# Dilated-convolution attention and a selective scan on one core: projection weights loaded a batch ahead into a second place, last-stage loads cut into 16 rows and one row, image margins cleared only

## The reference

```
# layer 0: four convolutions (1x1, and 3x3 with dilations 6, 12, 18), 32 channels each
branches = [relu(bn(conv(x, w, pad=p, dilation=d))) for w, p, d in ((w1,0,1),(w2,6,6),(w3,12,12),(w4,18,18))]
Q = wq . concat(branches) + bq      # 16 channels
K = wk . x + bk                     # 16 channels
V = wv . x + bv                     # 128 channels
Qn, Kn = Q/|Q|, K/|K|               # over channels
tailor = 1 / (N + Qn . (sum(Kn) + eps))
out = gamma * (sum(V) + Qn . (Kn V^T)) * tailor
# layer 1: on tokens x = out, D_MODEL 128, D_INNER 256, D_STATE 16
xh, z = split(x @ W_in);  xh = silu(causal_conv2(xh))
dt, Bm, Cm = softplus((xh W_x)[:8] W_dt + b_dt), (xh W_x)[8:24], (xh W_x)[24:40]
h = exp(dt*A) * h + dt*Bm*xh        # for each token, 256 x 16 states
y = (sum over states of h*Cm + xh*D) * silu(z)
y = silu(group_norm(y @ W_out, 4 groups)) + x
```

## Time and profile before

| | |
|---|---|
| median of 3 runs | 16281.83 us (16277.56 to 16301.75) |
| the profiled execution's own time | 16276.23 us |
| its span | 16274.4 us |
| busy: PE, DVE, POOL, ACT | 87%, 86%, 80%, 62% of the span |
| stage A, stages F and start of B, B, C | about 0 to 2440, to 2490, to 16157, to 16274 us |

### The profile page before, as it was taken

How to read it: one execution, slowest core, us unless ns; L and a number is a source line. 1 busy time by engine, 2 the same in 40 slices (tenths; PEclk the granted TensorE clock), 3 DMA queues, 4 the chain that set the end, 5 groups by cost and what they waited for, 6 DMA issues and landing times. The chain is left out here.

```text
span 16274.4 us, 144588 instructions
## 1 busy us (share of the span) xinstructions
PE 14161.2 (87%) x40704; PEld 5407.5 (33%) x40704; DVE 13974.3 (86%) x13537; ACT 10107.5 (62%) x14054; POOL 13069.0 (80%) x5647
## 2 busy tenths in 40 slices
PE   8999997888888888888888888888888888888886
PEld 3333332333333333333333333333333333333332
DVE  1222228999999999999999999999999999999997
ACT  2222225666666666666666666666666676666675
POOL 0000007999999999999999999999999999999996
PEclk9999998999999999999999999999999999999997
DMA  1111104444445545444455454454544444545544
GB/s 50 42 39 44 39 26 151 171 161 169 170 172 180 180 168 180 173 178 171 175 182 181 168 180 173 176 182 164 182 178 172 177 176 175 182 167 181 180 173 172
DMA packets 560359, 2505.37 MB, mean 154 GB/s; under 512 B 58695, under 2 KB 171063, under 8 KB 293448
## 3 DMA queue, kind: packets, MB, share of 16 engines
q1 hardware_dynamic: 549272, 2477.68, 42.9%
q10 hardware_dynamic: 10288, 18.44, 0.4%
HBM read 2325.32 MB, written 170.57 MB: 153 GB/s over the span
## 5 line engine op out<-in xcount | busy, mean ns | idle before, releaser
L794 POOL TENSOR_TENSOR hc<-h,c_all 128x1024 f32<-128x1024 f32 x4096 | 9531.7, 2359 | 574.0 <-DVE h L1161 496.1
L1031 PE MATMUL y_ps<-hc,ident 128*128 128x512 f32 x16392 | 8392.7, 664 | 1127.8 <-POOL hc L794 1127.6
L892 ACT ACTIVATE d_a<-dt,a_neg 128x512 f32<-128x512 f32 x8194 | 5596.1, 689 | 4081.4 <-DVE h L1161 4055.4
L1161 DVE TENSOR_TENSOR_SCAN h<-d_a,h,dbx_v 128x512 f32<-128x512 f32 x5456 | 6622.0, 1262 | 10.4 <-DVE dbx_v L1148 1.1
L1031 PEld LDWEIGHTS y_ps<-hc,ident 128*128 128x128 f32 x16392 | 3362.3, 211 | 6055.1 <-issue 4172.5
L1148 DVE TENSOR_TENSOR dbx_v<-dtx_ps,b_all 128x1024 f32<-128x1024 f32 x2816 | 3313.7, 1206 | 61.0 <-issue 26.2
L1161 DVE TENSOR_TENSOR_SCAN h<-d_a,h,dbx_p 128x512 f32<-128x512 f32 x2480 | 3027.7, 1262 | 10.8 <-issue 0.4
L783 POOL TENSOR_TENSOR dbx_p<-dtx,b_all 128x1024 f32<-128x1024 f32 x1280 | 3002.3, 2355 | 23.8 <-DVE h L1161 0.8
L480 POOL MEMSET ident_f<- 128x128 f32 x1 | 0.2, 205 | 2417.5 <-POOLq L45 2417.5
L273 PE MATMUL conv_ps<-image,w_taps 128*32 128x512 f32 x11520 | 1777.7, 594 | 0.0
L363 DVE RECIPROCAL k_inv<-k_nrm 128x4 f32<-128x4 f32 x256 | 45.5, 178 | 1774.2 <-ACT k_nrm L215 1774.2
(11 more groups left out here) (143 smaller groups left out, 9228.5 us busy)
## 6 DMA issues: line engine op xcount, KB each, us to landing
b_all<-bc_dram SPq DMA_DIRECT2D x1028, 1024.0 KB, 6.3
c_all<-bc_dram SPq DMA_DIRECT2D x1025, 1024.0 KB, 5.0
o_dram<-o_sb SPq DMA_DIRECT2D x257, 256.0 KB, 6.2
o_c<-o_dram SPq DMA_DIRECT2D x220, 256.0 KB
out<-r_c SPq DMA_DIRECT2D x220, 256.0 KB, 7.9
image<-in_x SPq DMA_DIRECT2D x91, 512.0 KB, 4.1
un<-un_dram SPq DMA_DIRECT2D x736, 34.0 KB
bc_dram<-low_bc SPq DMA_DIRECT2D x257, 64.0 KB, 4.6
```

Of the source, the lines that this page charges most:

```text
L794: nc.gpsimd.tensor_tensor(hc[:, n % HC], h[:, n], c_all[:, n // CG % 2, n % CG].unsqueeze(1).broadcast_to([128, 2, CH]), ALU.mult).then_in ...
L892: nc.scalar.activation(d_a[:, half], dt[:, p, half], ACT.Exp, scale=a_neg[:, half, n:n + 1]).then_inc(a_done, 1)
L1031: last = nc.tensor.matmul(y_ps[:, half], ident[:], hc[:, n % HC, half], start=False, stop=(n == S - 1))
L1161: nc.vector.tensor_tensor_scan(h[:, n, half], d_a[:, half], dbx, zero_col[:] if first else h[:, n, half, CH - 1:CH], ALU.mult, ALU.add).th ...
```

## The change

1. **Stage A, margins.** The clearing of the whole `image` becomes four clears: 18 rows above, 18 columns left, 18 columns right, 18 rows below. The four loads of the first image no longer wait for the clears.
2. **Stage A, waits.** PE's one wait per batch becomes several. In the first batch it waits for each of the four loads on a semaphore of its own, before chunks 0, 2, 10 and 18. In later batches it waits for the 13 pieces before chunk 0 and for the last 24 rows before chunk 20.
3. **Stage B, weights.** `w_xz` gets a second place, and the batches take turns. The second batch's weights are loaded in the first body. In the last body of batch b the weights of batch b+2 are loaded, into the place that batch b used. PE waits on one of two semaphores.
4. **Stage C, loads.** Each 17-row load becomes one of 16 rows and one of one row. Only the two batches' matrices are loaded instead of eight. The matrices and the first part of `u_t` are issued by ACT, ahead of its square root. SP issues two loads of `o_t` first, then the second part of `u_t`. The group norm's parameters get a semaphore of their own, so DVE no longer waits for the matrices.

```diff
-            sp.wait_ge(cleared, 6)
             for i in range(4):
                 rows = slice(i * 32, i * 32 + 32)
                 sp.dma_start(image[:, PAD + 32 * i:PAD + 32 * i + 32, PAD:PAD + W],
-                             t["x"][0, :, rows, :]).then_inc(x_loaded, 16)
-
+                             t["x"][0, :, rows, :]).then_inc(x_first[i], 16)
+
+            sp.wait_ge(cleared, CLEARED)
...
-                                 t["x"][b + 1, :, rest:H, :]).then_inc(x_loaded, 16)
+                                 t["x"][b + 1, :, rest:H, :]).then_inc(x_rest, 16)
...
-        def loaded(eng, b):
-
-            eng.wait_ge(x_loaded, 16 * 4 + b * (16 * (PIECES - 2)))
+        def loaded(eng, b, r):
+
+            if b == 0:
+                for i in range(4):
+                    if r == max(0, (32 * i - max(DIL) - ROWS) // ROWS):
+                        eng.wait_ge(x_first[i], 16)
+            elif r == 0:
+                eng.wait_ge(x_loaded, 16 * b * (PIECES - 3))
+            elif r == ((PIECES - 3) * PIECE - max(DIL) - ROWS) // ROWS:
+                eng.wait_ge(x_rest, 16 * b)
...
-            pool.memset(image[:], 0.0).then_inc(cleared, 1)
+            pool.memset(image[:, 0:PAD], 0.0).then_inc(cleared, 1)
+            pool.memset(image[:, PAD:PAD + H, 0:PAD], 0.0).then_inc(cleared, 1)
+            pool.memset(image[:, PAD:PAD + H, PAD + W:WP], 0.0).then_inc(cleared, 1)
+            pool.memset(image[:, PAD + H:WP], 0.0).then_inc(cleared, 1)
...
-        w_xz = sb("w_xz", [64 + KU, 2 * DI])
+        w_xz = sb("w_xz", [64 + KU, 2, 2 * DI])
...
-                if last:
-                    sp.dma_start(w_xz[0:K2], w_dram[bass.ds(b + 1, 1)].rearrange("o k c -> (o k) c")
-                                 ).then_inc(w_loaded, 16)
+                if km == 0:
+                    sp.dma_start(w_xz[0:K2, 1], w_dram[1]).then_inc(w_loaded[1], 16)
+                elif last and b + 2 <= B:
+                    sp.dma_start(w_xz[0:K2, b % 2], w_dram[b + 2]).then_inc(w_loaded[b % 2], 16)
...
-                after(pe, "w_loaded", 16 * batch + 16)
+                after(pe, f"w_loaded{batch % 2}", 16 * (batch // 2) + 16)
...
-        gm = sb("gm_c", [128, B, C])
+        gm = sb("gm_c", [128, 2, C])
...
+        def load_u(eng, i):
+
+            b, j0 = parts[i]
+            c0 = (b * SLOTS + 1) * CH
+            for g in range(groups):
+                for rows in (slice(0, M), slice(M, KU)):
+                    eng.dma_start(u_t[32 * g + rows.start:32 * g + rows.stop, i, j0:],
+                                  un_dram[rows, c0:c0 + N].rearrange("k (j g n) -> k j g n", g=groups, n=CH)[:, j0:, g]
+                                  ).then_inc(u_in[i], 16)
...
+            load_o(0)
+            load_o(1)
+            load_u(sp, 1)
+            for k in range(2, len(blocks)):
+                load_o(k)
...
+            for g in range(groups):
+                for rows in (slice(0, M), slice(M, KU)):
+                    act.dma_start(gm[32 * g + rows.start:32 * g + rows.stop],
+                                  gmat_dram[B - 2:B, rows].rearrange("b k c -> k b c")).then_inc(gm_in, 16)
+            load_u(act, 0)
             act.wait_ge(step, STEPS_BEFORE_ROOT)
```

More of the change, by code:

```diff
@@ L35 @@
 PIECES = H // PIECE
+CLEARED = 9
 HC = 4
@@ L98, in phase_a @@
         pads_stored = sem("pads_stored")
+        x_first = [sem(f"x_first{i}") for i in range(4)]
         x_loaded = sem("x_loaded")
+        x_rest = sem("x_rest")
         conv_done = sem("conv_done")
@@ L202, in _ @@
             act.wait_ge(set_up, 5)
-            act.wait_ge(cleared, 6)
+            act.wait_ge(cleared, CLEARED)
             def relu(b, r, p):
@@ L251, in _ @@
             pe.wait_ge(weights, 16 * 7)
-            pe.wait_ge(cleared, 6)
+            pe.wait_ge(cleared, CLEARED)
             pe.sem_inc(q_mm, 1)
@@ L299, in _ @@
             for b in range(0, B):
-                loaded(pe, b)
                 for r in range(NCH + 1):
@@ L305, in _ @@
                     if r < NCH:
+                        loaded(pe, b, r)
                         kv(b, r, p)
@@ L339, in _ @@
             nc.vector.tensor_tensor(bn_shift[:], bn[:, 1:2], bn_mi[:], ALU.subtract).then_inc(set_up, 1)
-            dve.wait_ge(cleared, 6)
+            dve.wait_ge(cleared, CLEARED)
             dve.sem_inc(v_done, 2)
@@ L599, in phase_b @@
         u_c = un[64:64 + KU]
-        gm_c = w_xz[64:64 + KU].rearrange("k (s c) -> k s c", c=C)
+        gm_c = w_xz[64:64 + KU, 0].rearrange("k (s c) -> k s c", c=C)
         d_a = ps("d_a", [128, 2, CH])
@@ L616, in phase_b @@
         weights, consts, ready, built = stage("weights"), stage("consts"), stage("ready"), stage("built")
-        w_loaded = stage("w_loaded")
+        w_loaded = [stage("w_loaded0"), stage("w_loaded1")]
         un_in = [stage("un_in0"), stage("un_in1")]
@@ L683, in _ @@
             load_un(2 * CH, 1)
-            sp.dma_start(w_xz[0:K2], w_dram[0]).then_inc(w_loaded, 16)
+            sp.dma_start(w_xz[0:K2, 0], w_dram[0]).then_inc(w_loaded[0], 16)
             after(sp, "rows_done", 1)
@@ L755, in _ @@
             after(sp, "bc_stored", 16 * (B * NCH + 1))
-            after(sp, "w_loaded", 16 * (B + 1))
+            after(sp, "w_loaded0", 16 * (B // 2 + 1))
+            after(sp, "w_loaded1", 16 * (B // 2))
             for p in range(2):
@@ L992, in inner, with gated @@
                 after(pe, "dt_done", km + 1)
-                nc.tensor.matmul(p_ps[:, 1 - half], w_xz[0:K2, 128 * half:128 * half + 128], un[0:K2, p],
+                nc.tensor.matmul(p_ps[:, 1 - half], w_xz[0:K2, batch % 2, 128 * half:128 * half + 128], un[0:K2, p],
                                  start=True, stop=True).then_inc(xh_mm[half], 1)
-            def gated(km, p, half):
+            def gated(km, batch, p, half):
                 after(pe, f"xh_silu{half}", km + 2)
-                nc.tensor.matmul(p_ps[:, 1 - half], w_xz[0:K2, DI + 128 * half:DI + 128 * half + 128], un[0:K2, p],
+                nc.tensor.matmul(p_ps[:, 1 - half], w_xz[0:K2, batch % 2, DI + 128 * half:DI + 128 * half + 128], un[0:K2, p],
                                  start=True, stop=True).then_inc(z_mm[half], 1)
@@ L1062, in _ @@
             inner(-1, 1, 0, 0, 1)
[L1063 to L1064 removed]
+            gated(-1, 0, 0, 0)
+            gated(-1, 0, 0, 1)
             project_x(-1, 0)
@@ L1078, in body @@
                 add_state(km - 1, 15)
-                gated(km, q, 0)
-                gated(km, q, 1)
+                gated(km, batch, q, 0)
+                gated(km, batch, q, 1)
                 add_skip(km, p)
@@ L1312, in phase_c, with load_o @@
         blocks = [(b, j, k) for k, (b, j) in enumerate(blocks)]
-        first_of = [sum(NCB - j0 for _, j0 in parts[:i]) for i in range(len(parts) + 1)]
         part_of = [i for i, (_, j0) in enumerate(parts) for _ in range(j0, NCB)]
         groups = CB // CH
+        def load_u(eng, i):
[6 more added lines that the diff above has]
+                                  ).then_inc(u_in[i], 16)
         @block.sync
         def _(sp):
-            sp.dma_start(gn[:], t["gn"]).then_inc(small_in, 16)
-            for g in range(groups):
-                sp.dma_start(gm[32 * g:32 * g + KU], gmat_dram.rearrange("b k c -> k b c")).then_inc(small_in, 16)
-            def load_u(i):
-                b, j0 = parts[i]
-                if i >= 2:
-                    sp.wait_ge(res_mm, first_of[i - 1])
-                c0 = (b * SLOTS + 1) * CH
-                for g in range(groups):
-                    sp.dma_start(u_t[32 * g:32 * g + KU, i % 2, j0:],
-                                 un_dram[:, c0:c0 + N].rearrange("k (j g n) -> k j g n", g=groups, n=CH)[:, j0:, g]
-                                 ).then_inc(u_in[i % 2], 16)
-            load_u(0)
-            for b, j, k in blocks:
-                s = k % CBUF
+            sp.dma_start(gn[:], t["gn"]).then_inc(gn_in, 16)
+            def load_o(k):
+                b, j, _ = blocks[k]
                 if k >= CBUF:
@@ L1337, in _ @@
                 c0 = (b * NCH + 1) * CH + j * CB
-                sp.dma_start(o_t[:, s], o_dram[:, c0:c0 + CB]).then_inc(o_in[s], 16)
-                if k == first_of[part_of[k]] and part_of[k] + 1 < len(parts):
-                    load_u(part_of[k] + 1)
+                sp.dma_start(o_t[:, k % CBUF], o_dram[:, c0:c0 + CB]).then_inc(o_in[k % CBUF], 16)
+            load_o(0)
[3 more added lines that the diff above has]
+                load_o(k)
         @block.scalar
@@ L1373, in _ @@
                 for g in range(groups):
-                    last = nc.tensor.matmul(res_ps[:, k % 2, CH * g:CH * g + CH], gm[32 * g:32 * g + KU, b],
+                    last = nc.tensor.matmul(res_ps[:, k % 2, CH * g:CH * g + CH], gm[32 * g:32 * g + KU, b - (B - 2)],
                                             u_t[32 * g:32 * g + KU, part_of[k] % 2, j], start=True, stop=True)
```

16 lines of the change are left out of this document (9 added, 7 removed).

## The result

The changed kernel takes 16055.5 us (median of 4 runs, 16041.7 to 16074.2) against 16286.0 (4 runs) of the kernel before on the same chip: a ratio of 0.9858, 95% interval 0.9841 to 0.9875. Its profiled execution took 16048.2 us, its span 16046.4, against 16276.2 and 16274.4.

| stretch | before | after | less | forecast |
|---|---|---|---|---|
| PE's first product starts at | 56.89 | 13.95 | 42.9 | 42.5 |
| from there to the first gate | 2466.8 | 2427.9 | 38.9 | 35 |
| first gate to last gate | 13628.6 | 13538.2 | 90.4 | 63 +- 20 |
| last gate to the end of the span | 122.1 | 66.4 | 55.8 | 63 |

What follows compares the result with a forecast made beforehand. Stage B was taken to run at the pace of DVE's loop, untouched, leaving late transfers to gain from. 42.5 + 35 + 63 + 63 = 203.5 us off 16276.2 gave 16073 us, range 16030 to 16115.

Steps and rivals of the forecast that it cites:

- the term without a sign: Stage B: whether ordinary chunks fall into the 52.38 or 52.88 us pattern after a batch's end, taken as +-20 us.
- Part 1: Start of stage A: PE's first product moves from 56.9 to 14.4 us, saving 42.5 us.
- Part 2: Batch ends in stage A: PE's image waits and the lower clock behind them go, 5.0 us for each of seven, 35.
- Part 3: Batch ends in stage B: the late `w_xz` no longer delays DVE's gate, six of 9.5 and two of 3, 63 us.
- Part 4: Stage C: faster loads and a new queue order end it at 211 on its scale, saving 63 us.
- The bound of three times the price for the column strips: Start of stage A: dearer GpSimd clears of the strips would add 7.7 us, and PE would start at 19.5.
- the upper end of my bounds: Batch ends in stage A: the saving was bounded by 25 us, if the clock still falls, and 39 us.
- Rival 1: Stage B gives only PE's waits, the gate staying late for clock or tokens: 34 us there, end 16102; chance 0.09.
- by then four blocks of `o_t` and `u_t` are through or in flight: Stage C, when the first SiLU ends near 172.5: only 14.7 MB are left, 34.5 us at 426 GB/s.
- Rival 3: Stage C stays slow, small loads and above all single rows holding up `u_t`: 32 us there, end 16104; chance 0.07.
- Rivals 4: Stage B: `w_xz` 2 KB longer moves later tiles and slows 256 chunks; at 1 us each, 16329; chance 0.02.
- rival 5: The change doesn't do what it says, at PE's `cleared` wait or the two places' turns: 16179; chance 0.03.

Runs made afterwards that it cites:

- the single later run: The changed kernel run once more with nothing edited; one run, 16073.4 us.
- b_places: The kernel before with only the second place for `w_xz` added; 16209.6 us, ratio 0.9956.
- b_head: The kernel before, single place for `w_xz`, its load moved to the head of SP's last body; 16204.5 us against 16289.4, ratio 0.9953.
- c_spread: The changed kernel with the last batch's `u_t` loads sent to partitions 8 apart, four single rows left out; 16061.5 us, ratio 0.9864.

## Why the prediction came out right, and where it did not

**Forecast.** 16073 us, range 16030 to 16115; measured 16055.5, and 16073.4 in the single later run. The sum was made for the profiled execution: 203.5 us forecast, 228.0 measured. Of the 24.5 between them 27.4 came from the term without a sign, 4.3 from parts 1 and 2, and 7.2 were lost in stage C. That the first and the last of these have opposite signs is luck. The mechanism was right in parts 1 and 2; in part 3 the wait was right and its cause was left open; in part 4 the cut did what it was meant to do, but one step failed.

**Part 1, the start.** 42.5 forecast, 42.9 measured, alone and together. The bound of three times the price for the column strips can go: they cost the contiguous price.

**Part 2, stage A's batch ends.** 35 forecast, 38.9 measured, 5.6 for each of seven, at the upper end of my bounds. The clock did not fall at all, and chunk 0 took 2.55 us less, where I had given 1.4.

**Part 3, stage B's batch ends.** 63 forecast. The eight chunks, 62.3 to 62.6 five times, 60.9 once, and 55.7 and 56.0, became ordinary ones of 52.3 to 53.5, 63 us against a mean of 52.74, and `b_places` alone gave 61.3. I said that the load "stands behind SP's queue". `b_head` confirmed it, and the counts show behind what: 2 us of issues, and on one engine the loads of 17 rows, 4.1 to 4.6 us. I put the shorter ends of the first and the eighth batch down to the missing store and load of finished output; the third 17-row load is missing there as well, and by the counts it is worth 1.2 to 1.8 us. Rival 1 is out: the wait for the transfer caused all of the 9.9 us, PE's lower clock and the gate's wait were its consequences.

**The term without a sign.** The 90.4 us in stage B were 63 and 27 from the ordinary mean. My +-20 was not quite enough; that it varies between executions of one kernel, and by about 25 us, I had not said.

**Part 4, stage C.** The step that failed is "by then four blocks of `o_t` and `u_t` are through or in flight". It took the rate of the earlier trace rows, measured on 128-partition tiles, for the 1.25 MB of `u_t`, which go to groups of 16 neighbouring partitions. While they came in, the engines moved 108 to 165 GB/s with their share at 1, so everything behind them waited too. The first product came 13.3 us after the last issue, and the stage saved 55.8 instead of 63. The 16 issues on ACT took 7.8 us instead of 5.4, which cost nothing: the scales were ready at 15996.8, 10 us ahead of `u_t`. Rival 3 expected slow small loads, but of another cause: it named the issues and the single rows. In `c_spread`, which kept 16-row loads of the same pieces, the rate doubled by the destination. That run left the four single rows out, so about 1 of its 6 us may be theirs, an estimate from 32 pieces at 0.31 us each over 8 to 16 engines. In the changed kernel all but three of the large part's 100 counts are in by 16005.83, so that its slowest engine costs 1.3 us at most.

**Rivals 4 and 5.** With tiles 2 KB further on, ordinary chunks took what they took (52.777 in `b_places` against 52.796), and both halves of rival 5 are denied by the waits above.

## What to carry to other kernels

When a load is late, look at what stands ahead of it in its queue before giving it a second buffer, and above all for loads that one engine carries alone: moving one issue gained the same 0.5%, and the 17-row loads that were the trouble in stage C held up `w_xz` in stage B as well. The change left those of stage B whole, and no run cut them. Count a load by the partitions it lands in, not only by its engines: here a busy share near 1 at a quarter of the usual GB/s meant that the engines waited for one another at the destination. And before moving an instruction to relieve one wait, read who waits for what it is moved behind.

## What the runs showed of the hardware

- Loads of 16 rows into 16 neighbouring partitions ran at 108 GB/s over all engines with 2 KB pieces (312 ns a piece), and at 122 with long rows; into 16 partitions 8 apart at 235 (149 ns a piece). One engine alone carried 25.
- Three loads of 17 rows (34 KB each), issued within 2 us, landed one behind the other, the last 9.8 us after its issue, and held up one of seven parts of the load behind them by 4.5 us.
- GpSimd's clear costs 0.88 ns an element in pieces of 18 and 0.87 in one piece.
- Sixteen instructions of 17 x 512 at the lower clock, 1.05 us each, end in 3.79 us over four groups of partitions (0.24 each); where neighbours share a group, sixty-one took 39.4 (0.65 each).
- Executions of one kernel differed by 25 us at the last gate, with nothing else in the profile changed but how often a chunk is the longer kind.
